# Local attention whose values are the stationary operand, with probabilities divided ahead of the product and a mask of 64 rows per bank

## What is computed

```
# six times, with 16 heads of 64 features, windows of 32 positions
q, k, v = split(shift_tokens(x) @ Wqkv)
q = rotary(l2norm(q) * qs); k = rotary(l2norm(k) * ks)
# each window of 32 queries sees its own 32 keys and the 32 before them
sim = einsum('bhwie,bhwje->bhwij', q, k2) * 8.0
sim = where(mask, -big, sim)            # causal within 32, nothing before position 0
attn = softmax(sim, -1)
out = einsum('bhwij,bhwje->bhwie', attn, v2) @ Wo
x = out + x
x = feed_forward(shift_tokens(x)) + x   # layer norm, 128 -> 2 x 341, gelu gate, 341 -> 128
```

## Time and profile of the kernel before

| | us |
|---|---|
| median of 3 runs | 2670.76 (2668.0 to 2670.93) |
| the profiled execution | 2668.14 |
| its span in the profile | 2666.4 |
| busy PE / DVE / ACT / POOL | 2461.7 / 2152.5 / 1983.0 / 1535.3 |
| granted TensorE clock, mean | 0.985 |

### The profile page before, as it was taken

The page is one execution under the profiler, slowest core; times in us unless marked ns, Lnnn a source line. Parts: engine busy times, 40 slices in busy tenths (PEclk is TensorE's granted clock), DMA queues, the critical chain, the costliest instruction groups (busy, mean ns, idle before and its releaser), DMA issues. The chain is left out here.

```text
span 2666.4 us, 118322 instructions
## 1 busy us (share of the span) xinstructions
PE 2461.7 (92%) x52349; PEld 1963.5 (74%) x52349; DVE 2152.5 (81%) x2452; ACT 1983.0 (74%) x3936; POOL 1535.3 (58%) x1072
## 2 busy tenths in 40 slices
PE   6799999999999999999999999679999999997999
PEld 2578788878777788788887787557777767775787
DVE  5788888888787888888887787388988988884888
ACT  4678888888787888888887787566767666664775
POOL 4788887888778778887887777022223222221110
PEclk8899999999999999999999999899999999998999
DMA  3233433343333333433342333031322222221221
GB/s 97 54 91 91 104 76 92 92 105 81 83 90 101 76 91 93 104 79 94 93 106 66 82 83 79 25 72 36 74 57 61 55 55 63 52 56 30 81 72 40
DMA packets 275775, 201.99 MB, mean 76 GB/s; under 512 B 117552, under 2 KB 215864, under 8 KB 274232
## 3 DMA queue, kind: packets, MB, share of 16 engines
q1 hardware_dynamic: 275264, 194.42, 29.8%
HBM read 36.96 MB, written 1.11 MB: 14 GB/s over the span
## 5 line engine op out<-in xcount | busy, mean ns | idle before, releaser
L506 POOL TENSOR_TENSOR lt_t_sin<-lt_qk,lt_tab 128x512 f32<-128x512 f32 x384 | 685.4, 1806 | 262.8 <-DVE lt_qk L1262 260.3
L511 POOL TENSOR_TENSOR lt_qr<-lt_qr,lt_t_sin 128x1024 f32<-128x1024 f32 x192 | 455.6, 2373 | 28.1 <-POOL lt_t_sin L506 0.9
L2031 DVE TENSOR_REDUCE fa_neg_max<-bank 128x1 f32<-128x1024 f32 x256 | 301.6, 1220 | 87.5 <-PE bank L1839 86.7
L1255 DVE TENSOR_REDUCE lt_ssq<-lt_qr 128x32 f32<-128x2048 f32 x96 | 219.4, 2286 | 143.4 <-ACT lt_qr L964 143.4
L1863 PE MATMUL bank<-fa_prob_t,fa_v 32*64 32x128 f32 x16384 | 280.7, 276 | 26.5 <-issue 21.7
L2041 DVE STREAM_TRANSPOSE fa_prob_t<-fa_prob 128x1024 f32<-128x1024 f32 x256 | 302.1, 1219 | 0.0
L1863 PEld LDWEIGHTS bank<-fa_prob_t,fa_v 32*64 32x64 f32 x16384 | 243.6, 131 | 73.1 <-issue 51.3
L1953 ACT ACTIVATE fa_prob<-bank,fa_neg_max 128x1024 f32<-128x1024 f32 x128 | 142.6, 1114 | 206.7 <-DVE fa_neg_max L2031 160.1
L597 PE MATMUL bank<-lt_w_high,lt_x_high 128*128 128x512 f32 x576 | 279.8, 486 | 1.7 <-ACT lt_v_tok L983 1.3
L1262 DVE TENSOR_TENSOR lt_qk<-lt_qk,lt_rn 128x2048 f32<-128x2048 f32 x96 | 233.0, 2427 | 34.7 <-ACT lt_rn L977 33.9
L614 PE MATMUL bank<-ident,lt_qr 128*128 128x128 f32 x1536 | 233.8, 276 | 27.9 <-ACT lt_q_t L998 19.0
(11 more groups left out here) (246 smaller groups left out, 5859.2 us busy)
## 6 DMA issues: line engine op xcount, KB each, us to landing
lt_v<-lt_v_tok SPq DMA_DIRECT2D x576, 128.0 KB
fa_v<-fa_v_tok SPq DMA_DIRECT2D x256, 128.0 KB, 2.6
lt_v<-lt_v_tok SPq DMA_DIRECT2D x192, 64.0 KB
lt_k_t<-lt_k_t SPq DMA_DIRECT2D x84, 128.0 KB, 2.7
lt_v<-lt_v SPq DMA_DIRECT2D x168, 64.0 KB, 2.0
lt_w_raw<-in_lt_wqkv_dram SPq DMA_DIRECT2D x36, 256.0 KB, 3.2
ex_cw_all<-cw_kept SPq DMA_DIRECT2D x8, 1024.0 KB, 4.7
lt_x_s<-h_in SPq DMA_DIRECT2D x96, 64.0 KB, 2.7
```

The source lines that it names most:

```text
L506: pool.tensor_tensor(dst[:, :, i, :], src[:, :, 1 - i, :], tab[:, g // 2 % 2, 1, at:at + 32].unsqueeze(1).to_broadcast([P, HEADS, 32]), AL ...
L511: pool.tensor_tensor(qr[:, g % 2, half], qr[:, g % 2, half], t_sin[:, :], ALU.add).then_inc(S.rotated, 1)
L2031: dve.tensor_reduce(neg_max[:, u % 2, par:par + 1], bank[:, 2 * par:2 * par + 2, :].rearrange("p a n -> p (a n)"), AX.X, ALU.max, negate=T ...
```

## The change

Values become the stationary operand (64 rows by 64 columns) and the transposed probabilities stream (32 columns). The product then has features in rows, as `project_out` needs it, so the transpose of the result and its use of the ring are gone. `empty_att` copies straight from the banks of the values, once per bank. Because positions are no longer in rows, the division by the row sums moves ahead of the transpose: `norm_probs` multiplies the 1024 probabilities of a row in one instruction, and `norm_att` is gone. The order of pairs in the result needs other rows of Wo, which are loaded by four DMAs per layer in place of one. The mask of blocks with earlier keys is a product of 64 rows per bank: the even bank by the upper half of the rows of a doubled identity, the odd bank by the lower half. The first two blocks of a layer (12 of 96) keep 128 rows.

```diff
@@ scores
-                        pe.wait_ge(S.av_out, 2 * (g - 2) + 1)
+                        pe.wait_ge(S.att_out, 2 * (g - 2) + 1)
                     for par in range(2):
-                        pe.matmul(bank[:, score_bank(g, par), :], ident_b[:, :], mask[:, 1 if has_look(g) else 0, :],
-                                  start=True, stop=False, skip_group_check=True)
+                        f = slice(64 * par, 64 * par + 64)
+                        if has_look(g):
+                            pe.matmul(bank[:, score_bank(g, par), :], half_b[f, :, :].rearrange("p a k -> p (a k)"), mask[f, :],
+                                      start=True, stop=False, skip_group_check=True)
...
@@ turn_prob
-                        pe.wait_ge(S.probs, 2 * (g + 1))
+                        pe.wait_ge(S.prob_normed, g + 1)
@@ weigh_v
-                        pe.wait_ge(S.av_out, 2 * g)
+                        pe.wait_ge(S.att_out, 2 * g)
                     if live(g + 1):
                         pe.wait_ge(S.shifted, 2 * (g + 1) + 1)
-                                mm = pe.matmul(bank[WIN * w:WIN * w + WIN, value_bank(g, par), hp * HD:(hp + 1) * HD],
-                                               prob_t[f, g % 2, hp, WIN * w:WIN * w + WIN],
-                                               v[f, g % 2, w, hp, :], start=True, stop=True)
+                    for hp, w, par in ((2 * j + m, w, par) for j in range(PAIRS // 2) for w in range(WPB)
+                                       for m in range(2) for par in range(2)):
+                                to, at = 64 * ((par + hp) % 2), hp // 2 * BLK + WIN * w
+                                mm = pe.matmul(bank[to:to + 64, value_bank(g, par), at:at + WIN], v[f, g % 2, w, hp, :],
+                                               prob_t[f, g % 2, hp, WIN * w:WIN * w + WIN], start=True, stop=True)
@@ order on ACT
                 for i in STEPS:
+                    if live(i - 2):
+                        empty_att(i - 2, 0)
                     for j in range(4):
                         if live(i):
                             empty_turned(i, j)
...
-                    if live(i - 2):
-                        empty_att(i - 2, 0)
-                        empty_att(i - 2, 1)
+                        if live(i - 2) and j == 0:
+                            empty_att(i - 2, 1)
@@ on DVE
-                def norm_att(g, par):
...
+                def norm_probs(g):
+                    heads = prob[:, g % 2, :, :, :].rearrange("p h a k -> p (h a) k")
+                    dve.wait_ge(S.inv_sum, g + 1)
+                    dve.tensor_tensor(heads, heads, row_sum[:, g % 2, :].unsqueeze(2).to_broadcast([P, HEADS, HD]), ALU.mult)\
+                       .then_inc(S.prob_normed, 1)
...
                     if live(i + 1):
                         normalise(i + 1)
+                    if live(i - 1):
+                        sum_probs(i - 1)
+                        norm_probs(i - 1)
+                    if live(i + 1):
+                        rotate_cos(i + 1)
...
-                        norm_att(i - 1, 0)
...
-                        norm_att(i - 1, 1)
```

More of the change, by code:

```diff
@@ L96, in time_mixing_and_local @@
         tab = buf("tab", [P, 2, 2, 2 * HD])
-        mask = buf("mask", [P, 2, PAIRS * HD], BF16)
+        mask_first = buf("mask_first", [P, HD], BF16)
+        mask = buf("mask", [P, PAIRS * HD], BF16)
         ident_b = buf("ident_b", [P, P], BF16)
+        half_b = buf("half_b", [P, 2, 64], BF16)
         center_w = buf("center_w", [P, P])
@@ L133, in time_mixing_and_local @@
                  "proj proj_out v_proj v_out squared sumsq clamped ln inv_norm normed rot_cos rot_sin rotated "
-                 "turned turn_out scores rowmax shifted probs rowsum inv_sum prob_turned prob_out av av_out "
-                 "att_turned att_out out out_done f_mean f_squared f_var f_ln f_rstd f_scaled f_normed up gated "
+                 "turned turn_out scores rowmax shifted probs rowsum inv_sum prob_normed prob_turned prob_out av "
+                 "att_out out out_done f_mean f_squared f_var f_ln f_rstd f_scaled f_normed up gated "
                  "hidden down ff_out last_x last_mean last_squared last_var last_ln last_rstd last_scaled last_out").split()
@@ L269, in time_mixing_and_local @@
                     uses["qk", i + 2, j] = len(uses)
-            if live(i - 2):
-                uses["att", i - 2, 0] = len(uses)
-                uses["att", i - 2, 1] = len(uses)
             if i - 2 == ALL - 1:
@@ L327, in wait_layer @@
         def wait_layer(eng, layer):
-            eng.wait_ge(s_layer[layer % 2], 64 * (layer // 2 + 1))
+            eng.wait_ge(s_layer[layer % 2], 112 * (layer // 2 + 1))
         with nc.Block(no_gpsimd_drain=True) as blk:
@@ L343, in load_layer @@
                         sp.wait_ge(S.ff_out, BLOCKS * (layer - 1))
-                    dst = (w_1[:, r, :], w_2[:, r, :, :], lvec[:, r, :], w_o[:, r, :, :])[i]
-                    sp.dma_start(dst, A[("lt_w1", "lt_w2", "lt_vec", "lt_wo")[i]][layer]).then_inc(s_layer[r], 16)
+                    if i < 3:
+                        dst = (w_1[:, r, :], w_2[:, r, :, :], lvec[:, r, :])[i]
+                        sp.dma_start(dst, A[("lt_w1", "lt_w2", "lt_vec")[i]][layer]).then_inc(s_layer[r], 16)
+                        return
+                    for par in range(2):
+                        for half in range(2):
+                            f, src = slice(64 * half, 64 * half + 64), slice(64 * par, 64 * par + 64)
+                            sp.dma_start(w_o[f, r, 4 * par:4 * par + 4, :], A["lt_wo"][layer][src, (par + half) % 2::2, :])\
+                              .then_inc(s_layer[r], 16)
                 def load_scale(layer, i):
@@ L540, in _ @@
                 pool.tensor_copy(ident_b[:, :], ident[:, :]).then_inc(S.cast, 1)
+                pool.tensor_tensor(half_b[:, :, :], ident[:, 0:64].unsqueeze(1).to_broadcast([P, 2, 64]),
+                                   ident[:, 64:P].unsqueeze(1).to_broadcast([P, 2, 64]), ALU.add).then_inc(S.cast, 1)
                 pool.wait_ge(S.mask, 16)
-                for i in range(2):
-                    pool.tensor_copy(mask[:, i, :].rearrange("p (a k) -> p a k", a=PAIRS),
-                                     mask_f[:, i:i + 1, :].to_broadcast([P, PAIRS, HD])).then_inc(S.cast, 1)
+                pool.tensor_copy(mask_first[:, :], mask_f[:, 0, :]).then_inc(S.cast, 1)
+                pool.tensor_copy(mask[:, :].rearrange("p (a k) -> p a k", a=PAIRS),
+                                 mask_f[:, 1:2, :].to_broadcast([P, PAIRS, HD])).then_inc(S.cast, 1)
                 split_low(0)
@@ L1263, in normalise, with rotate_cos @@
                        .then_inc(S.normed, 1)
+                def rotate_cos(g):
                     dve.wait_ge(S.normed, g + 1)
```

47 lines of the change are left out of this document (11 added, 36 removed).

## The result

The changed kernel takes 2788.43 us (median of 4 runs, 2771.45 to 2800.55), the kernel before 2670.85 (2668.0 to 2675.89): ratio 1.0434, 95% interval [1.0374, 1.0493], +117.6 us. The direction was forecast, the size was not: 2719 us was predicted, and the time lies just above the range. The profiled execution took 2771.45 us, 2769.7 of it in the span, so it is the fastest of the four; its difference from the profiled one before is 103.3 us.

What follows compares the result with a forecast made beforehand. A loop through ACT, as long as PE's own work, was taken to bound the kernel. A pair +1.81 us, 46 pairs +83, less 21 and 14, net +48 on the median 2670.8: 2719 us, range 2645 to 2785.

Steps and rivals of the forecast that it cites:

- The ruler and the loop: ACT's step L973, first of three making 1/norm, times each block; PE's 92% hides a loop through ACT as long.
- PE's own work: A gain: transposes -0.87, masks -0.19, values product +0.38, sum -0.68 us a block, counting only if PE sets the pace.
- The slack behind it: Behind the up block's values product, PE reaches the third group of transposes 1.1 us before ACT lets it start.
- ACT's order: A loss in the down block: result copies move ahead of q and k copies, way to the mask 0.65 us longer.
- DVE's order: The larger loss, in the up block: DVE's new chain takes 9.91 us, plus stalls of 1.06 and 0.3 us.
- The stall of the division: In the up block, DVE's division of the probabilities waits 1.06 us for POOL's sine products.
- L1262's delay by POOL: POOL's remaining work runs into the next block's L1262, DVE's first product, by 0.1 to 0.5 us a pair, taken as 0.3.
- What comes off: Two deductions: -21 us for waits inside the values product, mostly vanishing in PE's slack; -14 us for L1262's present loss to POOL.
- No stall on DVE: Rival: the division slips between POOL's two products, or POOL starts late; about -14 us, 2657 us; chance 0.19.
- PE's pace: Rival: PE sets the pace, so its 65 us come out whole, 2606 us, or half, 2640; chance 0.16.
- The slow product: Rival: values product takes 5.0 us, loads and streams all in turn; 133 us over 46 pairs, 2852 us; chance 0.05.
- The mask does what it says: Rival denied here: the two mask products run in turn as before; 0.19 us in the down half, 9 us; no chance given.

## Why the prediction was right or wrong

**What bounds the kernel.** The ruler and the loop were right: most of the loss is where ACT waits for DVE before `shift_norm`, in the up half.

**PE's own work.** The masks went from 0.59 to 0.39 us as said, and the transposes' 0.87 us vanished; no run shows a gain from them. The values product was put at 1.8 us and takes 2.00. The rule of the Trainium skill weighed there ("TensorE: Matmul & The Clock Gate", "The mechanism"), taken strictly, would have made it 5.0; the trace does not agree for these tiles. The slack behind it was overrated. (Its sum is also off by 0.1: 10.8 + 8.97 = 19.8 and not 19.9.) The claim that up to about 3 us hides rested on the distance to the next transposes, and did not look at the up products that stand between, for which ACT waits. The doubled product came at 80% of its 3.5 us a block.

**ACT's order.** The way to the mask in the down block was worked out as 5.38 us; it is 1088.76 - 1083.39 = 5.37. From the transposes of the probabilities to the next ruler 5.93 were carried over, and 1098.52 - 1092.59 = 5.93. Only the piece between was 3.83 us and not 4.37, in part because the pair read before held a wait of PE for itself that was taken for work (0.24 of the 0.54 us; the rest is not explained):

```profile
928.21 1.56 PE L718 MATMUL bank<-lt_f_gate,lt_w 128*128 128x256 f32 x6 [0.24 <-issue]
```

So the down half was put at 15.68 and is 15.14.

**DVE's order: the step that failed.** The stall of the division was put at 1.06 us, and 2.21 - 1.15 = 1.06 is what the row shows; 85 of the 96 take over 2.1 us. But "by 0.1 to 0.5 us once a pair; I take 0.3", L1262's delay by POOL, is the term that was mis-sized. It is 3.87 - 2.29 = 1.58 us in the pair shown, 1.28 more than taken, and about that in most of the 20 up halves behind a `w_low`; in the other 25 it is 0.43 (median), inside the stated bounds. With 1.58 the predicted 18.95 us of the up half become 20.23, and 20.11 was measured in that pair; with 0.43 they become 19.08, and 18.98 was measured in the other pair shown.

Two things were left out of the term. One is `w_low`: POOL's remaining work was listed as 2.38 + 2.50 + 2.38 us, and in these pairs 1.28 us more stand in the same queue. They stood there before the change, just ahead of the earlier trace rows:

```profile
1094.48 1.28 POOL L474 TENSOR_TENSOR lt_w_low<-lt_w_raw,lt_w_high 128x512 fp32r<-128x512 f32 x1
```

The other is the down block's own stall. The collision was counted in the up block and then forgotten; in the down half 5.93 us was carried over as unchanged, and it was, but the same stall happened there too, off ACT's path, and POOL handed it on to the next L1265. The run with every second inverse in PSUM measures it: 1.0 of the 1.58. Had the rows of the shared steps been added up, it would have shown: from the earlier trace rows, 2.28 + 2.29 + 2.50 + 2.38 + 2.50 + 2.38 = 14.33 us, with `w_low` 15.61, already over a down half of 15.2, and with the division's 1.15 16.76. The rule of the Trainium skill ("SBUF — State Buffer", "SBUF: two separate sides") was cited rightly, and the inverse sums in PSUM agree with its condition of two SBUF inputs: 1.22 us for 2.21.

**What comes off.** Neither deduction came. The values product's waits for nothing shown were 20.9 us and are 22.1. And the 14 us of L1262 belonged to the old kernel's mean, where the pair chosen (32.82 us) stood 0.42 below the mean pair (33.24); a better pair would have needed no correction. The 35 us taken off should have been none.

**The size of the miss.** The time is 69 us above the 2719. The deductions are 35 of them. The pair was put at 1.81 us more and has 2.24, which is 20: the mean up half is 20.10 us for 18.95, 53 us too few in 46 pairs, in part made up by the down half, put at 15.68 for a mean of 15.43, and by the pair before, read 0.42 shorter than the mean. The last 14 are the distance from the profiled execution, the fastest of the four, to the median, and go with the lower clocks of the other three.

**The clock** had no term: a gap of 1.8 us on PE was not foreseen, so its half clock wasn't either. By the filled gap it is worth 18 us (medians) to 28 (ratios).

**The rivals.** No stall on DVE: refuted by L1305. PE's pace: the idle before the transposes grew only to 37.8 us, which alone would have spoken for it, but PE's idle moved before the values product instead, where the prediction didn't look. The slow product: 2.00, not 5.0. The mask does what it says.

**What stays open.** Without the stalls the change still costs 15 us (1.0055). The median down half is 0.23 us longer than before and the up half 0.13. ACT's copies ahead of q and k may hold part of it: moving one of them back takes 0.48 off the median down half and gives 0.47 back in the up half, and the whole time falls by 13 us by the medians and 9 by the ratios, with intervals that still touch (1.0038 to 1.0077 and 1.0009 to 1.0041). What the slower values product holds of it was not separated.

## What to carry to other kernels

Where two engines exclude each other, add up every operation of both that takes the shared thing, over one period, before moving or adding one, and do it for each sort of period: here a POOL operation of 1.28 us that comes in some blocks only decided how much of a stall came through. An engine busy 48% and one busy 82% can together be full for part of the time, and work added there is then paid far from where it stands; how much of it is paid depends on the room in each period (some 1.8 us of the two stalls' 2.0 a pair here, 33 us of 109 for the product added in another place). An operand moved from SBUF to PSUM takes an operation out of that sum, but look at who still reads the bank it moves into. Take the period from the mean over many blocks, not from one pair with corrections for the rest.

## What was not expected of the hardware

- A stall of 1.0 us is handed on undiminished over a whole block, where POOL's queue has no room in between: from the down block's division (1088.10) to the L1265 at 1099.49. In the up halves without a `w_low` ahead 0.43 us of it arrive.
- PE's clock fell 15 times where its gaps before the values product are no longer than 1.82 us in most blocks: 64.8 us at half clock, against 10.2 when the gap was filled. Eight of the falls came right behind such a gap; what led to the others stays open.
- 128 pairs of 64x64 weight load and 64x32 product take 2.00 us, 15.6 ns a pair, where 64x32 loads with 64 columns took 1.41, 11 ns. Twice as many in a row take 5.54 us, with 1 to 2 us of waits that nothing in the profile explains.
